# Deformable convolution: corner sums and 32x32 block turns on VectorE, products of six or seven tiles at once on TensorE, and a wait of GpSimd for all landings ahead of slot 0

## The reference

```python
off = conv3x3(groupnorm(x3), offset_w)                # 18 channels: (dy, dx) of 9 taps
sy, sx = base_y + off[:, :, 0], base_x + off[:, :, 1]
y0, x0 = floor(sy), floor(sx); ly, lx = sy - y0, sx - x0
p  = corner(y0,     x0,     (1 - ly) * (1 - lx))      # gathered pixel times its weight
p += corner(y0,     x0 + 1, (1 - ly) * lx)
p += corner(y0 + 1, x0,     ly * (1 - lx))
p += corner(y0 + 1, x0 + 1, ly * lx)
out = sum over 9 taps and 64 channels of deform_w * p
```

## Time and profile before

| | us |
|---|---|
| median of 3 runs | 14692.38 (14690.25 to 14722.44) |
| the profiled execution, own time | 14656.86 |
| its span, first to last instruction | 14654.9 |
| first gather starts / last gather starts | 3867.1 / 14601.9 |
| PE busy | 8240.4 (56%) |
| POOL busy | 7483.2 (51%) |
| DVE busy | 6540.2 (45%) |
| ACT busy | 2973.2 (20%) |

### The profile page before, as it was taken

One profiled execution on the slowest core, in us unless ns is written; L12 is line 12 of the kernel. 1 busy time (PEld: TensorE's weight loads), 2 busy tenths in 40 slices (PEclk: granted clock), 3 DMA queues, 4 the chain that ended last, 5 costly groups with the idle time before them and its releaser, 6 DMA issues.

```text
span 14654.9 us, 154001 instructions
## 1 busy us (share of the span) xinstructions
PE 8240.4 (56%) x51639; PEld 5651.9 (39%) x51639; DVE 6540.2 (45%) x13232; ACT 2973.2 (20%) x5102; POOL 7483.2 (51%) x7657
## 2 busy tenths in 40 slices
PE   6887888889453535444454535354444545353533
PEld 2333444449343433333333434343333333343433
DVE  5655555553235343434344353434343443534343
ACT  3433444433111111111111111111111111111111
POOL 0011222222366666666566666666666666666665
PEclk9998899999676767666676767666666767676766
DMA  3322111117333333333333333333333333333332
GB/s 91 88 81 71 53 57 53 61 47 228 100 97 110 99 107 102 113 94 113 98 107 110 97 108 97 109 103 112 94 113 95 113 109 98 109 97 106 103 96 83
DMA packets 503966, 1436.58 MB, mean 98 GB/s; under 512 B 128981, under 2 KB 234197, under 8 KB 474577
## 3 DMA queue, kind: packets, MB, share of 16 engines
q0 software_dynamic: 353344, 970.88, 22.5%
q1 hardware_dynamic: 150032, 458.00, 10.4%
HBM read 1175.46 MB, written 252.90 MB: 97 GB/s over the span
## 4 chain that ended last, share of the span: by engine, by line
another core or an unknown queue 38%; PE 16%; issue 12%; DVE 3%; ACT 3%; POOL 2%; DMA 0%; ACTq 0%; DVEq 0%; POOLq 0%; SPq 0%
PE e_ps L1939 9%; PE e_ps L1930 3%; POOL e_g L1783 2%; ACT e_corners L1846 2%; PE e_ps L1878 1%; PE e_ps L1889 1%; PE e_ps L1904 1%; DVE e_sty L2099 1%; DVE e_g L2090 1%; DVE e_g L2092 1%; DVE e_big L2112 0%; DVE e_x3t L1964 0%; DMA e_g<-table_dram,e_index_slots 0%; ACT e_pad L1820 0%
## 5 line engine op out<-in xcount | busy, mean ns | idle before, releaser
L1783 POOL DMA_INDIRECT e_g<-table_dram,e_index_slots x7056 | 6787.9, 962 | 4077.6 <-issue 2012.1
L1939 PE MATMUL e_ps<-e_corners,e_w_def 128*64 128x128 f32 x14112 | 2585.5, 358 | 4504.9 <-ACT e_corners L1846 3118.6
L1939 PEld LDWEIGHTS e_ps<-e_corners,e_w_def 128*64 128x64 f32 x14112 | 2280.0, 187 | 4790.6 <-ACT e_corners L1846 3282.8
L1930 PE MATMUL e_ps<-k_ident,e_g 128*128 128x128 f32 x7056 | 1281.1, 327 | 1263.0 <-DVE e_g L2092 654.7
L1846 ACT ACTIVATE e_corners<-e_ps 128x512 f32<-128x512 f32 (+1 forms) x2352 | 1027.0, 489 | 3253.4 <-remote 2383.7
L2060 DVE COPY e_index_slots<-e_index_now 128x9 uint32<-128x9 uint32 x784 | 141.3, 181 | 3272.9 <-DMA e_g<-table_dram,e_index_slots 3222.1
L1930 PEld LDWEIGHTS e_ps<-k_ident,e_g 128*128 128x128 f32 x7056 | 969.2, 168 | 1585.1 <-issue 899.5
L2089 DVE TENSOR_TENSOR e_ps<-e_g,e_ps 128x512 f32<-128x512 f32 (+1 forms) x2352 | 1327.0, 564 | 120.9 <-DMA e_g<-table_dram,e_index_slots 58.5
L1852 ACT ACTIVATE e_big<-e_ps 64x128 f32<-64x128 f32 x784 | 212.6, 271 | 5706.3 <-remote 4282.0
L2092 DVE TENSOR_TENSOR e_g<-e_g,e_ps 128x512 f32<-128x512 f32 (+1 forms) x2352 | 1301.1, 553 | 110.7 <-remote 12.2
L2090 DVE TENSOR_TENSOR e_g<-e_g,e_ps 128x512 f32<-128x512 f32 (+1 forms) x2352 | 1283.6, 546 | 0.0
(11 more groups left out here) (438 smaller groups left out, 8421.3 us busy)
## 6 DMA issues: line engine op xcount, KB each, us to landing
e_g<-table_dram,e_index_slots POOLq DMA_INDIRECT x7056
table_dram<-e_rt SPq DMA_DIRECT2D x32, 1624.0 KB
a_xt<-x_in SPq DMA_DIRECT2D x16, 1568.0 KB
v_dram<-a_vout SPq DMA_DIRECT2D x32, 784.0 KB, 8.5
b_xt<-v_dram SPq DMA_DIRECT2D x16, 1568.0 KB
v_dram<-b_vout SPq DMA_DIRECT2D x32, 784.0 KB, 7.7
c_v2t<-v_dram SPq DMA_DIRECT2D x16, 1568.0 KB
c_xt<-x_in SPq DMA_DIRECT2D x16, 1568.0 KB, 6.5
```

What stands on the lines that cost most here:

```text
L1783: pool.indirect_dma_start(out=g[:, slot, tap * CORNERS:(tap + 1) * CORNERS], out_offset=None, in_=table, in_offset=bass.IndirectOffsetOnAx ...
L1930: mm = pe.transpose(ps[:, TURN[tap // 4], (tap % 4) * P:(tap % 4 + 1) * P], g[:, slot, tap * CORNERS:tap * CORNERS + 2 * C], k.ident[:, :])
L1939: mm = pe.matmul(ps[0:C, OUT, 0:P], w_d[:, tap, :], corners[:, tap, :], start=(tap == 0), stop=(tap == TAPS - 1))
```

## The change

GpSimd issues the same gathers, in the same order. Its wait for the slot is now on VectorE's sums (`added`) in place of TensorE's transposes. Ahead of slot 0 of each round it waits as well for all landings of the round before.

VectorE multiplies the left side of all nine taps at once, and then goes through three batches of 3 taps: the right side's multiplication, the sum left + right of the upper neighbour (`joined`), of the lower one, the sum upper + lower (`added`), and a transposition of the 128x192 result in blocks of 32x32 into `turned` (`summed`). So the data of 4 quarters of 32 pixels stands with 32 channels on each group of 32 partitions.

TensorE has no transposes and no `corners` any more. It multiplies a **block** of 7 or 6 tiles (`BOUNDS`: 8 blocks for a pair) in 18 steps of 4 matmuls. Each of the four works on 32 partitions (one quarter of the pixels), with 32x128 weights (64 output channels twice) and 224 or 192 columns, into a PSUM bank of its own. ScalarE then copies a block with a few instructions; `big` has the two images on the two halves of the partitions.

The preparation stands between blocks on TensorE and ScalarE, with 6 PSUM banks in turn where there were 2, and `finish` of pair p stands between tiles 4 to 6 of pair p + 1, on 128 partitions in place of 64. The first pair stands outside of the loop.

The core of the diff:

```diff
+    BATCHES = tuple((lo, lo + 3) for lo in range(0, TAPS, 3))
+    BOUNDS = (0, 7, 13, 19, 25, 31, 37, 43, PX_TILES)
+    BLOCKS = tuple(zip(BOUNDS, BOUNDS[1:]))
+    FINISH_AT, X3_AT, X3_SUM_AT, STATS_AT, MOMENTS_AT, SCALE_AT, POSITIONS_AT = 4, 8, 10, 11, 13, 15, 34
+    MEANS_BLOCK, ROWS_BLOCK, OFFSETS_BLOCK, TURN_BLOCK = 1, 2, 3, 4
...
                 with pool.Fori(1, PAIRS * GROUPS) as r:
                     for slot in range(SLOTS):
-                        pool.wait_ge(bank_done, (r - 1) * (3 * SLOTS) + (3 * slot + 3))
+                        pool.wait_ge(added, (r - 1) * (3 * SLOTS) + (3 * slot + 3))
+                        if slot == 0:
+                            pool.wait_ge(gathered[SLOTS - 1], r * (16 * TAPS))
                         pause(pool, index_ready, r * SLOTS + (slot + 1), passed)
                         gather(slot)
...
+                def block_products(p, n):
+                    lo, hi = BLOCKS[n]
+                    wide = (hi - lo) * QUARTER
+                    pe.wait_ge(summed, p * (3 * PX_TILES) + 3 * hi)
+                    need(pe, out_ready, p * len(BLOCKS) + n)
+                    for step_ in range(TAPS * 2):
+                        for q in range(4):
+                            rows = slice(q * QUARTER, (q + 1) * QUARTER)
+                            mm = pe.matmul(ps[:, OUT[q], 0:wide], w_d[rows, step_, :], turned[rows, n % 2, step_, 0:wide],
+                                           start=(step_ == 0), stop=(step_ == TAPS * 2 - 1))
                     mm.then_inc(out_done, 1)
...
+                    if at_tile == lo:
+                        need(dve, out_done, p * len(BLOCKS) + (block - 1))
                     dve.wait_ge(gathered[slot], r * (16 * TAPS) + 16 * TAPS)
...
+                    dve.tensor_tensor(left, left, spread(0, TAPS, 0), ALU.mult).then_inc(weighted, 1)
+                    for n, (a, b) in enumerate(BATCHES):
+                        upper, lower = left[:, a:b, 0, :], left[:, a:b, 1, :]
+                        half = ps[:, HALF, 0:(b - a) * 2 * C].rearrange("p (k n c) -> p k n c", n=2, c=C)
+                        need(dve, summed, t * 3 + n)
+                        dve.tensor_tensor(half, sides[:, a:b, 1, :, :], spread(a, b, 1), ALU.mult).then_inc(weighted, 1)
+                        dve.wait_ge(weighted, t * 4 + (n + 2))
+                        dve.tensor_tensor(upper, upper, half[:, :, 0, :], ALU.add).then_inc(joined, 1)
+                        dve.tensor_tensor(half[:, :, 1, :], lower, half[:, :, 1, :], ALU.add).then_inc(joined, 1)
+                        dve.wait_ge(joined, t * 6 + (2 * n + 2))
+                        dve.tensor_tensor(half[:, :, 0, :], upper, half[:, :, 1, :], ALU.add).then_inc(added, 1)
+                        dve.wait_ge(added, t * 3 + (n + 1))
+                        dve.transpose(to.rearrange("p (k h) x -> p k h x", h=2),
+                                      half[:, :, 0, :].rearrange("p k (h x) -> p k h x", x=QUARTER)).then_inc(summed, 1)
...
+                def pair(p, behind, ahead):
+                    for at_tile in range(PX_TILES):
+                        turn(p, at_tile, ahead is None)
+                        if behind is not None and FINISH_AT <= at_tile < FINISH_AT + 3:
+                            finish(behind, at_tile - FINISH_AT)
+                        if ahead is not None:
+                            between(ahead, at_tile)
+                    if ahead is not None:
+                        switch(ahead)
```

More of the change, by code:

```diff
@@ L1863, in _ @@
+                prepare(0)
+                pair(0, None, 1)
+                with act.Fori(1, PAIRS - 1) as p:
+                    pair(p, p - 1, p + 1)
+                pair(PAIRS - 1, PAIRS - 2, None)
+                finish(PAIRS - 1)
             @block.tensor
@@ L1948, in _ @@
+                prepare(0)
+                pair(0, 1)
+                with pe.Fori(1, PAIRS - 1) as p:
+                    pair(p, p + 1)
+                pair(PAIRS - 1, None)
             @block.vector
@@ L2032, in hand_over @@
                     pause(dve, table_stored, n * 32 + 32, passed)
[L2033 removed]
+                    if isinstance(n, int) and n == 0:
                         switch(0)
@@ L2123, in build @@
+                pair(0, None, 1)
+                with dve.Fori(1, PAIRS - 1) as p:
+                    pair(p, p - 1, p + 1)
+                pair(PAIRS - 1, PAIRS - 2, None)
+                for part in range(3):
+                    finish(PAIRS - 1, part)
 def build(nc, io):
```

363 lines of the change are left out of this document (169 added, 194 removed).

## The result

| | before | changed |
|---|---|---|
| median, us | 14704.29 (4 runs) | 15022.86 (14965.96 to 15033.36, 4 runs) |
| ratio | | 1.0208, 95% interval 1.0179 to 1.0237 |
| span of the profiled execution | 14654.9 | 15022.3 |
| PE, DVE, POOL busy | 8240, 6540, 7483 | 6813, 8192, 7503 |

A forecast was written before the change was run, and what follows sets the result against it. GpSimd's gather stream, paused by waits for TensorE, was taken as the bound: 3867 ahead + 8905 gathers + 276 landing waits + 50 finish + 480 TensorE + 50 tail = 13,628, forecast median 13,665 us, range 13,030 to 14,640.

The forecast's parts named there:

- What bounds the kernel: Deform phase: GpSimd's gather stream, paused by a TensorE slowed beside gathers to about an instruction per us.
- Waits on `added`: GpSimd's wait for VectorE's sums: a tile costs VectorE 7.4 us, gathers 11.36, so GpSimd does not wait.
- the prediction's cover: VectorE beside the gathers: it keeps up with a pair's 577 us as long as a tile takes at most 11.1 us.
- case E: VectorE binds: from 11.1 us a tile it sets the pace, from 13.0 it is slower than before; chance 0.03.
- The landing wait: GpSimd ahead of slot 0: 111 pauses of 2.5 us, 276 us in all, each giving TensorE 10 fast us.
- B: Rival: the short pause does not free TensorE, each block ends in a stall; 14,641 us, about no change; chance 0.17.
- D: Rival: TensorE's four 32-row matmuls run one after another, a block 28 us; 14,930 up to 18,500 us; chance 0.11.
- The term of 480 us: TensorE's shortage in slow stretches stalls GpSimd: 30 us a pair, 480 us in all, from 0 to 1056.
- The tail: Behind the last gather's end: last tile, block, copies and shorter finish; 50 us, where it was 52.1.
- C: Rival: gathers do not slow TensorE, its exchange with ScalarE did; nothing is short, 13,185 us; chance 0.08.
- the 1831 us of waits: GpSimd's waits between gathers in the kernel before, 114 us a pair, taken as what can be won.
- my floor: GpSimd's 7056 gathers at 1.262 us each, 8905 us, taken as unchanged and not reducible.

The follow-up runs named there:

- two_steps: Changed kernel with 2 of the 18 steps of each block's products (8 matmuls in place of 72), all else kept; 14338.82 us, ratio 0.9755.
- rest_slot04: Changed kernel with a long GpSimd memset (3000 elements) ahead of slots 0 and 4 of each round, landing wait kept; 14979.37 us, ratio 1.0190.
- the two kernels of 8 and 48 elements: Changed kernel with a GpSimd memset of 8 or 48 elements behind every gather; 15110.19 us (1.0252) and 15090.73 us (1.0239).

## Why the prediction was wrong

- **What bounds the kernel.** The reading of the earlier trace rows was half of it. TensorE is slow beside gathers and fast without, but not by an instruction per us while GpSimd streams. In the slow steps an instruction starts 0.70 or 1.40 us, or a longer step of that grid, after the one that it depends on, on VectorE as on TensorE. Counted over the deform phase, 716 starts of matmuls and weight loads follow the one ahead by 0.70 or 1.40 us (within 0.06) in the kernel before and 4046 in the changed one. A sign for VectorE was in the trace of the kernel before, in its first run of 81 gathers, and I passed it over:

```profile
3946.59 0.29 DVE L2092 TENSOR_TENSOR e_g<-e_g,e_ps 128x128 f32<-128x128 f32 x1 [1.21 <-DVE e_g L2090]
```

- **Waits on `added`.** The tile is 7.4 us in good time, as summed, and the transposition that no row showed is 0.382 us, the low bound. "GpSimd, seven tiles ahead, does not wait for it" is the step that failed: it waited 726.6 us for the sums and 1241.7 within the stream for the indices that VectorE puts down. The pace of VectorE was taken from good stretches. In slow steps its chain of dependent instructions, three batches of four, makes up to 24 us of 7.4, twice a tile of gathers. Summed over the phase a tile took 10.9 us (8572 us for 784), just under the 11.1 of the prediction's cover. What takes it over is the wait ahead of the copies of the indices, 1410.2 us or 88 a pair, for TensorE for the most part: by an estimate a pair of VectorE has 49 x 10.9 + 35 + 88 = 657 us, over the 577 of the gathers. This was case E together with TensorE's lateness, and by another way than the transposition; slow tiles have no term in the sum.
- **The landing wait.** Its own price was right (2.64 us against 2.8, less 0.30). That it gives TensorE 10 good us, the largest uncertainty named, was wrong for this short pause, and B right; behind a stall of 7.5 us it had 17 good us (8702.6 to 8720). B's 14,641 is too low by 380 us, since it too left VectorE at 7.4 us.
- **TensorE.** The four matmuls side by side were right: a block in good time took 6.1 us (8548.84 to 8554.97), 6.9 were forecast and 9.0 by the factor of 3.07, so D fell. The term of 480 us is the mis-sized one: `two_steps` puts 684 us on the products alone, and the 1177 us of VectorE and the preparation stand beside that. From first to last gather are 11,089 us, where 8905 + 276 + 50 + 480 = 9711 were predicted: 1378 us too few. The tail adds 22 to the miss, an earlier first gather and the median, which lies at the profiled execution's own time here and not 35.5 above it, take some 43 back: 1358 in all, 15,023 for 13,665.
- **The tail** was 72 us from the last gather's end, where 50 were forecast: VectorE was behind, and ScalarE took the last block at 15005.08, 55 us after the last gather.
- **C**, gathers do not slow TensorE, fell by the two windows and the timeline above. The rule of the Trainium skill ("SBUF — State Buffer") that TensorE waits for no one there isn't disproved; but who reads it as "gathers cost TensorE nothing" is wrong here by what the windows show.
- **The range**, 13,030 to 14,640, held the shortage of TensorE and nothing for VectorE; 15,023 lay beyond it.

Why the kernel before is well off without being spaced: it spaces itself. Restarts of GpSimd behind its pauses, timeline of the kernel before:

```profile
4007.37 0.94 POOL L1783 DMA_INDIRECT e_g<-table_dram,e_index_slots  x1 [3.98 <-remote]
...
4033.64 0.95 POOL L1783 DMA_INDIRECT e_g<-table_dram,e_index_slots  x1 [4.05 <-remote]
4059.95 0.95 POOL L1783 DMA_INDIRECT e_g<-table_dram,e_index_slots  x1 [4.06 <-remote]
```

Eighteen gathers in 26.3 us are 1.46 a gather, and over the phase the median tile comes after 13.3 us, 1.48 a gather. In the changed kernel half of the tiles come at 1.28 or less, and long stalls follow: its mean of 1.57 is higher, but in bursts. So the 1831 us of waits that I counted as the prize are by an estimate for the most part the price of the spacing: at 1.446, the spacing of the fastest kernel here, 7056 gathers take 10,203 us, where 8905 was my floor.

**Open.** What takes 1.40 us was not seen, nor whether it is one for each gather. Each execution on record has a recorded span and clock, so nothing here tells whether recording takes part in it. Not tried was a VectorE tile with fewer dependent instructions, nor how the loss splits between VectorE and the preparation, since `two_steps` kept both. `rest_slot04` does not stand in order in the table, nor do the two kernels of 8 and 48 elements; why two long rests are worse than a little after each tile at nearly the same mean isn't settled. Even gaps and one gap behind nine gathers were not run at the same mean spacing, so a small difference between them could hide.

## What to carry to other kernels

A wait on an engine that streams DMAs may be what keeps the others fast. Before removing it, look for starts that lie on a grid, and at the mean spacing of the stream with and without the wait, not only at the work. When one engine's stream slows what all others wait for, a short filler behind each burst can be worth more than the rearrangement: here a memset of 1.1 us a tile took the changed kernel without its landing wait from 1.0139 to 0.9679.

## What was not expected of the hardware

In the kernels whose gathers GpSimd issued 1.25 to 1.42 us apart on average, steps of TensorE and VectorE that depend on an earlier instruction fell onto a common grid of 0.70 us, with 1.40 for most on VectorE and 2.1 or 2.8 between matmuls. On VectorE it set in 42 us after the first gather at a pitch of 1.25, was nearly gone at 1.43 and not seen at 1.45. On TensorE it was still there at 1.45 (blocks of 33 us on average) and in part at 1.47 (20 us), and gone in the kernel with 1.44 from gather to gather and 1.56 over all (11 us). It was the same with half of the bytes at the same pitch, and with half of the rows at a pitch of 1.20.
